# Two transformer layers on one core: compact value blocks, a reordered first group, and layer 0's scores taken bank by bank

## The chip, the cores and the metric

The kernel runs on one core of a Trainium2 chip. The metric is the time of the whole program on the device in microseconds; lower is better. All data starts in device memory and the result ends there.

## The reference, cut to what matters

`x` is 4 batches of 512 rows of width 128; the context has 77 rows per batch. There are 16 heads of width 8 in both cross-attentions.

```python
x = x + xattn0(layernorm(x), ctx, ctx, mask)   # softmax over 77 keys, mask fill -1e8, projections q k v o with biases
x = x + ffn0(layernorm(x))                     # attention over the 4 batches (4 heads), then 8 experts, top-1 gate, capacity 256
x = x + xattn1(layernorm(x), ctx, ctx)         # keeps the 32 largest scores of each row, softmax over them; v is ctx itself
x = x + ffn1(layernorm(x))                     # r * (relu(k)^2 @ Wv), inputs shifted by one row
# in both cross-attentions, for each head:
scores = q @ k.T / sqrt(8)
out = softmax(scores) @ v
```

## The kernel before

The 2048 rows of `x` are 16 tiles of 128 rows. The program has stages that follow one another on all engines:

1. Preparation. Weights and constants come in by DMA. Keys for both cross-attentions are projected (L925, L926) and spread into block-diagonal form: `kblk` holds, in each group of 32 partitions (four heads of width 8), four blocks of 77 columns, so that one matmul over 32 partitions gives the scores of four heads, 308 columns, one PSUM bank. Values are spread too: the 16 x 77 = 1232 pairs of head and key are cut into ten chunks of 128 rows, and `vblk[chunk]` is a 128 x 144 block, 128 columns for the output and 16 for the softmax denominators, zero except in the columns of the two or three heads that the chunk's rows belong to. ScalarE writes the transposed context sixteen times over (L415), TensorE multiplies each 128-column piece of it with all of Wv or transposes it (L937, L939), VectorE multiplies with a head mask (L627), twelve times for each layer. Then layer 1's mixing weights are made (L633 to L638).
2. Layer 0, cross-attention and feed-forward attention with gating, in four groups of four tiles (one of each batch). Each engine has its own program; all of them follow one list of step names, `GROUP_ORDER`, and each takes from it the steps that it has. The list is written out by hand. Steps of `attend` are of group j, steps of `among` of group j-1. Semaphores order the engines; an engine's queue runs strictly in its order. The first group also holds `w12a`, `w12b` (products w1 w2 of the eight experts, 64 TensorE records) and `b12` (64 records).
3. A hand-over, and then the 16 tiles one by one: experts, layer 1's query, top-32 on VectorE (L866, L877), weighing on GpSimd and ScalarE, the value product (L1168), layer 1's feed-forward. It is a software pipeline in the order of `TILE_ORDER`; value runs two tiles behind the top-k, mix three.

A tile of layer 0's cross-attention goes thus (names are those of the list, b is the tile in the group):
- `s` (L971, L974): four score matmuls, one for each bank, each on its own 32 partitions; then four more that add the mask row (65 partitions, bf16) to the four banks.
- `mx` (L671): one VectorE maximum over all four banks, 1232 columns.
- `sub` (L676): one VectorE subtraction from PSUM into `d0` in SBUF. The next tile's `s` waits for it.
- `exp` (L435): one ScalarE exponential from `d0` into `e0`, which scales by 1/sqrt(8).
- `ta`, `tb`, `tc` (L988): ten TensorE transposes, copied to SBUF by ScalarE (`ca` L440, `cc` L444, L445) and VectorE (`cb` L683).
- `v` (L998): ten value matmuls into one PSUM bank, fp32, which are 20 TensorE records; `nm` (L688, L691) divides by the denominators; `ot`, `oT`, `op` transpose and project (L1003, L450, L1007); `x` (L697) adds to the residual. `v` of a tile waits for `x` of the one before, since they share the bank.

In the list `hstats`, `hrstd`, `hnorm`, `hturn`, `hT`, `hq`, `hqT` are the layer norm of four tiles (L643, L646, L282, L653), its transposes (L951), and the query projection (L962). `q`, `qs`, `qk`, `dot`, `soft`, `wv`, `tot`, `res`, `ynorm` and `gate` are the feed-forward attention of the group before, mostly on VectorE. Steps for GpSimd in the list are `hrstd`, `bias`, `zrstd`, `zbias`, `xbias`, `yrstd`, `yaffine`, `ystore`.

SP's queue carries the input DMAs in order: context, weights, columns, mask, x, rows, biases, w1; and w2 only when the context area that it overwrites is free (L253).

## Time and profile before

| | us |
|---|---|
| median of 3 runs | 688.25 (688.17 to 688.58) |
| profiled execution, first to last instruction | 689.4 |
| PE busy | 455.3 (66%) |
| DVE busy | 512.7 (74%) |
| ACT busy | 291.1 (42%) |
| POOL busy | 263.1 (38%) |

The page gives for the profiled execution its span, and no time of its own around it. PE is TensorE's matmuls, PEld its weight loads, DVE is VectorE, ACT ScalarE, POOL GpSimd, SP the engine that issues most DMAs. The second part of the page is the span in 40 slices of 17.2 us; a digit is the busy share in tenths, PEclk the granted TensorE clock (9 is full):

```profile
PE   3759958747765777685678776775666748455445
...
DVE  3644446966956963759989999979889799999800
ACT  3002222223222232443656677774656547553342
...
PEclk9978977988897897766778888886887788665555
```

The waits and the chain of the page are read by stage, not for the whole, since the stages have different limits. "From start to start" below is how far apart two instructions of one engine begin; durations overlap, so it is often less than the duration.

### The profile page before, as it was taken

To read this page: it belongs to the slowest core of one execution; us is meant where nothing else is said; L and a number is where in the kernel's file an instruction comes from. 1 tells how busy PE (TensorE), PEld (TensorE's weight loads), DVE (VectorE), ACT (ScalarE), POOL (GpSimd) and SP (SyncE) were. 2 spreads that over 40 slices of the span, in tenths; PEclk is the share of its full clock that TensorE was granted. 3 is DMA by queue.
4 is the path that set the end of the run, shared out by engine and by line. 5 is a ranking of instruction groups with operands and counts; after the bars stand their busy time and mean duration, and the time that the engine had idled before them with its cause. 6 is when DMAs were issued, how large, how long until landed. Compare 5 with 4: busy or idle time off the path is not lost. (4 is left out here: it accounts for less than half of the span.)

```text
span 689.4 us, 11334 instructions
## 1 busy us (share of the span) xinstructions
PE 455.3 (66%) x2460; PEld 338.7 (49%) x2460; DVE 512.7 (74%) x3078; ACT 291.1 (42%) x789; POOL 263.1 (38%) x404
## 2 busy tenths in 40 slices
PE   3759958747765777685678776775666748455445
PEld 2727744544652664353445554553455436444334
DVE  3644446966956963759989999979889799999800
ACT  3002222223222232443656677774656547553342
POOL 4010030032023022332556765655546646645442
PEclk9978977988897897766778888886887788665555
DMA  8030000000000000000000000000000000000000
GB/s 323 9 122 1 1 0 1 2 0 2 0 1 0 0 0 1 0 0 1 0 1 1 6 5 5 6 1 4 6 1 4 5 4 1 4 4 6 4 4 8
DMA packets 3816, 9.42 MB, mean 14 GB/s; under 512 B 808, under 2 KB 2992, under 8 KB 3376
## 3 DMA queue, kind: packets, MB, share of 16 engines
q1 hardware_dynamic: 3616, 7.96, 3.1%
q10 hardware_dynamic: 144, 0.88, 0.3%
q14 instruction: 42, 0.34, 0.2%
q8 instruction: 14, 0.23, 0.1%
HBM read 7.79 MB, written 1.05 MB: 13 GB/s over the span
## 5 line engine op out<-in xcount | busy, mean ns | idle before, releaser
L866 DVE MAX8 top<-area_b 128x8 f32<-128x77 f32 x768 | 112.1, 228 | 0.0
L877 DVE MATCH_REPLACE8 area_b<-top,area_b 128x77 f32<-128x77 f32 x512 | 106.9, 229 | 0.0
L374 POOL TENSOR_TENSOR e<-area_b 128x1232 f32<-128x1232 f32 x16 | 44.7, 2797 | 43.2 <-issue 23.0
L1168 PEld LDWEIGHTS psM<-vblk,pT 128*128 128x128 f32 (+1 forms) x320 | 54.3, 241 | 9.3 <-issue 9.3
L1154 PE MATMUL psT<-consts,e 128*128 128x128 f32 (+1 forms) x160 | 33.2, 331 | 38.6 <-POOL e L374 25.6
L1168 PE MATMUL psM<-vblk,pT 128*128 128x144 f32 (+3 forms) x320 | 53.7, 336 | 0.0
L877 DVE MATCH_REPLACE8 area_b<-top,area_a 128x77 f32<-128x77 f32 x256 | 53.5, 233 | 0.0
L998 PE MATMUL psM<-vblk,pT 128*128 128x144 f32 (+1 forms) x320 | 48.7, 314 | 6.8 <-DVE x L697 6.2
L362 POOL TENSOR_TENSOR d<-area_a,mxc 128x1232 f32<-128x1232 f32 x16 | 36.0, 2248 | 41.3 <-DVEq L893 41.3
L998 PEld LDWEIGHTS psM<-vblk,pT 128*128 128x128 f32 (+1 forms) x320 | 46.2, 214 | 8.8 <-ACT pT L445 5.3
L282 POOL TENSOR_TENSOR rstd_m<-veps_m,expo 128x4 f32<-128x4 f32 x8 | 8.4, 1050 | 109.9 <-DVE veps_m L648 109.9
L866 DVE MAX8 top<-area_a 128x8 f32<-128x77 f32 x256 | 37.4, 226 | 16.7 <-issue 10.9
L515 ACT ACTIVATE consts<-psM,cur 128x128 f32<-128x128 f32 x128 | 38.2, 369 | 17.5 <-PE psM L1116 17.5
L1154 PEld LDWEIGHTS psT<-consts,e 128*128 128x128 f32 (+1 forms) x160 | 19.7, 160 | 50.5 <-POOL e L374 26.1
L877 DVE MATCH_VALUE_LOAD area_b<-top,area_b 128x8 f32 x512 | 44.2, 86 | 0.0
L1116 PE MATMUL psM<-w,y1T 128*128 128x512 f32 (+1 forms) x64 | 35.6, 647 | 6.3 <-ACT consts L515 6.1
L671 DVE TENSOR_REDUCE mx<-psS 128x16 f32<-128x1232 f32 x16 | 23.0, 1438 | 21.5 <-PE psS L974 21.5
L282 POOL TENSOR_TENSOR rstd_x<-veps_x,expo 128x4 f32<-128x4 f32 x4 | 4.1, 1025 | 90.6 <-DVE veps_x L648 90.6
L1124 PE MATMUL psM<-consts 128*128 128x128 f32 x288 | 38.1, 291 | 0.0
L1124 PEld LDWEIGHTS psM<-consts 128*128 128x128 f32 x288 | 37.1, 209 | 0.0
L435 ACT ACTIVATE e<-d 128x1232 f32<-128x1232 f32 x16 | 19.7, 1231 | 39.4 <-DVE d L676 39.4
L367 POOL TENSOR_TENSOR area_b<-area_a,mxc 128x1232 f32<-128x1232 f32 x16 | 36.0, 2248 | 0.0
(212 smaller groups left out, 1130.9 us busy)
## 6 DMA issues: line engine op xcount, KB each, us to landing
area_a<-in_w1T SPq DMA_DIRECT2D x1, 2048.0 KB, 14.7
area_b<-in_w SPq DMA_DIRECT2D x1, 2048.0 KB, 8.2
x<-in_x SPq DMA_DIRECT2D x1, 1024.0 KB, 9.4
out<-fin SPq DMA_DIRECT2D x16, 64.0 KB, 1.5
consts<-in_consts ACTq DMA_DIRECT2D x1, 862.0 KB, 5.0
weights<-in_weights SPq DMA_DIRECT2D x1, 836.0 KB, 6.5
rows<-in_rows SPq DMA_DIRECT2D x1, 576.0 KB, 11.3
ctx_sb<-in_ctxT SPq DMA_DIRECT2D x1, 154.0 KB, 4.7
```

What stands on the lines that cost most here:

```text
L362: e.tensor_tensor(dif[:], scores_sb[par][:], mxc[:, 0, :, None].broadcast_to([P, H, KEYS]), ALU.subtract)\
L367: e.tensor_tensor(cut, scores_sb[par][:], mxc[:, 1, :, None].broadcast_to([P, H, KEYS]), ALU.subtract)\
L374: e.tensor_tensor(p1.rearrange("p (h k) -> p h k", k=KEYS), ex1, cut, ALU.mult).then_inc(s["p_set"], 1)
L515: ins = e.activation(mparts[:, x_], psM0[:, at + (x_ - lo) * D:at + (x_ - lo + 1) * D], ACT.Copy, scale=cur[:, D + x_:D + x_ + 1])
L671: e.tensor_reduce(mx0.rearrange("p (g i) -> p g i", g=G), scores_ps, AX, ALU.max).then_inc(s["s_max"], 1)
L866: ins = e.max(top[:, r, h], (left if r else scores_sb[par])[:, h])
L877: ins = e.match_replace(left[:, h], top[:, r, h], (left if r else scores_sb[par])[:, h], GONE)
L998: ins = mm(psM0[:, 0:VW], pT[0:w, c], vblk0[0:w, b, c], start=(c == 0), stop=(c == NCH - 1))
L1116: mm(psM0[:, 0:(hi - lo) * D], y1T[:], w12[:, lo:hi].rearrange("p e n -> p (e n)"), start=True, stop=True)\
L1124: ins = mm(psM0[:, 0:D], ident, mparts[:, x_], start=False, stop=(x_ == E))
L1154: ins = tr(psT[0:w, 0, (c % 4) * P:(c % 4 + 1) * P], p1[:, c * P:c * P + w], ident)
L1168: ins = mm(psM1[:, 0:VW], pT1[0:w, c], vblk1[0:w, t // NJ, c], start=(c == 0), stop=(c == NCH - 1), skip_group_check=True)
```

## The change

- `vblk1` is made on the host and comes by DMA. `vblk0` has 27 columns a chunk for 144: three heads of 8 columns and a denominator column each (`FIRST` says which heads). It is made by 40 matmuls of 24 columns from the context, which comes three times over, and four VectorE maskings. The value products of both layers write 27 columns at the chunk's place in the bank.
- The first group of the list takes in the rest of the preparation: `masks`, `kblk`, `vb`, `vm`, `kblk1`, `wmix`, and w12 and b12 in eight pieces each. x comes in four DMAs, the first tile of each batch first; the weights in two parts.
- In every group of layer 0, `s`, `mx` and `e` are steps for each bank: one score matmul and its mask matmul, a negated maximum of four heads, four exponentials of 77 columns that read PSUM with the maximum as bias and write SBUF. `sub` and `d0` as its target are gone; `e0` alternates with the old `d0`. The factor 1/sqrt(8) is in the keys. A bank's scores wait for the exponentials of the same bank of the tile before.
- The list is a new one.

```diff
-VW = D + H
+VC = 3
+VE = HD + 1
+VW = H * VE
+VB = VC * VE
+REP = 3 * KEYS
+FIRST = [min(c * P // KEYS, H - VC) for c in range(NCH)]
+SHIFT = [c * P % KEYS for c in range(NCH)]
...
-    e.dma_start(cols[:], cols_d).then_inc(s["weights_in"], 16)
+    xt = x1.rearrange("p (b j) d -> p b j d", b=B)
+    xd = x.rearrange("p (b j) d -> p b j d", b=B)
+    e.dma_start(xt[:, :, 0], xd[:, :, 0]).then_inc(s["x_in"], 16)
+    e.dma_start(early[:], early_d).then_inc(s["early_in"], 16)
+    e.dma_start(cols[:], cols_d).then_inc(s["early_in"], 16)
     e.dma_start(mask_u8[:], mask.broadcast_to([P, B * KEYS]).rearrange("p (b k) -> p b k", b=B)).then_inc(s["mask_in"], 16)
-    e.dma_start(x1[:], x).then_inc(s["x_in"], 16)
-    e.dma_start(rows[:], rows_d.broadcast_to([P, sum(ROWS.values())])).then_inc(s["x_in"], 16)
+    e.dma_start(rows[:], rows_d.broadcast_to([P, sum(ROWS.values())])).then_inc(s["rows_in"], 16)
+    for j in range(1, NJ):
+        e.dma_start(xt[:, :, j], xd[:, :, j]).then_inc(s["x_rest"], 16)
     e.dma_start(b1T[:], b1T_d).then_inc(s["b_in"], 16)
     e.dma_start(b2[:], b2_d).then_inc(s["b_in"], 16)
+    e.dma_start(weights[:], weights_d).then_inc(s["weights_in"], 16)
     e.dma_start(w1T, w1T_d).then_inc(s["w1_in"], 16)
-    e.wait_ge(s["v_turned"], 2 * B * 3)
     e.dma_start(w2, w2_d).then_inc(s["w2_in"], 16)
...
-            def exp():
-                hold(e, s["s_sub"], u + 1)
-                hold(e, s["t_turned"], 3 * u)
-                e.activation(e0[:], d0.rearrange("p h k -> p (h k)"), ACT.Exp, scale=SCALE).then_inc(s["s_exp"], 1)
+            def exp(g):
+                def f():
+                    hold(e, s["s_max"], G * u + g + 1)
+                    if g == 0:
+                        hold(e, s["t_turned"], 3 * u - 3)
+                    for i in range(HG):
+                        h = HG * g + i
+                        ins = e.activation(e0s[b % 2][:, h * KEYS:(h + 1) * KEYS], scores_ps[:, g, i], ACT.Exp, bias=mx0[:, h:h + 1])
+                    ins.then_inc(s["s_exp"], 1)
...
-                        blk[:, :, None].broadcast_to([P, HG, KEYS]), ALU.mult).then_inc(s["kblk0_made"], 1)
-    for n in range(2 * B * 3):
-        v, b, g = (vblk0, vblk1)[n // (3 * B)], n // 3 % B, n % 3
-        lo, hi = 4 * g, min(4 * g + 4, NCH)
-        e.wait_ge(s["v_turned"], n + 1)
-        e.tensor_tensor(v[:, b, lo:hi, 0:D], psT[:, n % 2, 0:(hi - lo) * P].rearrange("p (c n) -> p c n", n=P),
-                        headmask[:, lo:hi, 0:D], ALU.mult).then_inc(s["v_masked"], 1)
-
...
-                hold(e, s["s_made"], u + 1)
-                hold(e, s["s_sub"], u)
-                e.tensor_reduce(mx0.rearrange("p (g i) -> p g i", g=G), scores_ps, AX, ALU.max).then_inc(s["s_max"], 1)
-
-            def subtract():
-                hold(e, s["s_max"], u + 1)
-                hold(e, s["s_exp"], u)
-                e.tensor_tensor(d0.rearrange("p (g i) k -> p g i k", g=G), scores_ps,
-                                mx0.rearrange("p (g i) -> p g i", g=G)[:, :, :, None].broadcast_to([P, G, HG, KEYS]),
-                                ALU.subtract).then_inc(s["s_sub"], 1)
+            def highest(g):
+                def f():
+                    hold(e, s["s_made"], G * u + g + 1)
+                    e.tensor_reduce(mx0[:, HG * g:HG * g + HG], scores_ps[:, g], AX, ALU.max, negate=True).then_inc(s["s_max"], 1)
+                return f
 
...
+            def masks():
+                e.wait_ge(s["mask_in"], 16)
+                e.tensor_copy(mask_f[:], mask_u8[:]).then_inc(s["mask_cast"], 1)
+                e.wait_ge(s["mask_cast"], 1)
+                e.wait_ge(s["constants_set"], 5)
+                for n, f in enumerate(fill_parts()):
+                    e.tensor_scalar(mrow[32 * n:32 * n + 1], mask_f[32 * n:32 * n + 1], -f, f, ALU.mult, ALU.add)\
+                        .then_inc(s["mrow_made"], 1)
+
+            def blocks():
+                e.wait_ge(s["k0_copied"], 1)
+                e.scalar_tensor_tensor(k0[:], k0[:], SCALE, mask_f[:], ALU.mult, ALU.mult).then_inc(s["k0_masked"], 1)
+                e.wait_ge(s["k0_masked"], 1)
+                e.wait_ge(s["consts_in"], 16)
+                for b in range(B):
+                    e.tensor_tensor(kblk0[:, b], k0[:, b, None, :].broadcast_to([P, HG, KEYS]),
+                                    blk[:, :, None].broadcast_to([P, HG, KEYS]), ALU.mult).then_inc(s["kblk0_made"], 1)
+
+            def values(b):
+                def f():
+                    e.wait_ge(s["v_turned"], b + 1)
+                    e.tensor_tensor(vblk0[:, b].rearrange("p c (i n) -> p (c i) n", n=VE)[:, :, 0:HD],
+                                    vbank[b % 2][:, 0:NCH * VC * HD].rearrange("p (n d) -> p n d", d=HD),
+                                    vmask, ALU.mult).then_inc(s["v_masked"], 1)
+                return f
...
     e.wait_ge(s["consts_in"], 16)
-    for n in range(2 * B * 3):
-        b, g = n // 3 % B, n % 3
-        e.wait_ge(s["ctx_rep"], b + 1)
-        if n >= 2:
-            e.wait_ge(s["v_masked"], n - 1)
-        for c in range(4 * g, min(4 * g + 4, NCH)):
-            dst = psT[:, n % 2, (c % 4) * P:(c % 4 + 1) * P]
-            if n < 3 * B:
-                ins = mm(dst, ctxrep[:, b, c * P:(c + 1) * P], Wt["wv0"], start=True, stop=True)
-            else:
-                ins = tr(dst, ctxrep[:, b, c * P:(c + 1) * P], ident)
-        ins.then_inc(s["v_turned"], 1)
...
 
-            def scores():
-                hold(e, s["h_qT"], j + 1)
-                hold(e, s["s_sub"], u)
-                for g in range(G):
+            def scores(g):
+                def f():
+                    if isinstance(u, int) and u == 0 and g == 0:
+                        e.wait_ge(s["kblk0_made"], B)
+                        e.wait_ge(s["mrow_made"], 3)
+                        e.wait_ge(s["constants_set"], 4)
+                    hold(e, s["h_qT"], j + 1)
+                    hold(e, s["s_exp"], G * u - G + g + 1)
                     mm(psS[:, g, 0:GW], q0T[32 * g:32 * g + 32, b], kblk0[32 * g:32 * g + 32, b].rearrange("p i k -> p (i k)"),
                        start=True, stop=False)
-                for g in range(G):
-                    ins = mm(psS[:, g, 0:GW], mones[:], mrow[:, b].rearrange("p i k -> p (i k)"), start=False, stop=True)
-                ins.then_inc(s["s_made"], 1)
+                    mm(psS[:, g, 0:GW], mones[:], mrow[:, b, None, :].broadcast_to([65, HG, KEYS]), start=False, stop=True).then_inc(s["s_made"], 1)
+                return f
 
...
-                    ins = mm(psM0[:, 0:VW], pT[0:w, c], vblk0[0:w, b, c], start=(c == 0), stop=(c == NCH - 1))
+                    ins = mm(psM0[:, FIRST[c] * VE:FIRST[c] * VE + VB], pT[0:w, c], vblk0[0:w, b, c], start=(c == 0),
+                             stop=(c == NCH - 1), skip_group_check=True)
                 ins.then_inc(s["pv_made"], 1)
 
...
-            def merged(n):
+            def spread(b):
                 def f():
-                    e.wait_ge(s["w1_in"], 16)
-                    e.wait_ge(s["w2_in"], 16)
-                    hold(e, s["w12_stored"], n)
-                    for x_ in range(4 * n, 4 * n + 4):
-                        for c in range(FC):
-                            ins = mm(psM1[:, (x_ % 4) * D:(x_ % 4 + 1) * D], w1T[:, c, x_], w2[:, c, x_], start=(c == 0), stop=(c == FC - 1))
-                    ins.then_inc(s["w12_made"], 1)
+                    if b == 0:
+                        e.wait_ge(s["k1_copied"], 1)
+                    if b >= 2:
+                        e.wait_ge(s["v_masked"], b - 1)
+                    for c in range(NCH):
+                        ins = mm(vbank[b % 2][:, c * VC * HD:(c + 1) * VC * HD], ctx_sb[:, b, SHIFT[c]:SHIFT[c] + P],
+                                 Wt["wv0"][:, FIRST[c] * HD:(FIRST[c] + VC) * HD], start=True, stop=True)
+                    ins.then_inc(s["v_turned"], 1)
                 return f
 
...
+            def merged(x_):
+                def f():
+                    if x_ == 0:
+                        e.wait_ge(s["w1_in"], 16)
+                        e.wait_ge(s["w2_in"], 16)
+                        e.wait_ge(s["v_masked"], B)
+                    if x_ == 4:
+                        e.wait_ge(s["w12_stored"], 1)
+                    for c in range(FC):
+                        ins = mm(psM1[:, (x_ % 4) * D:(x_ % 4 + 1) * D], w1T[:, c, x_], w2[:, c, x_], start=(c == 0), stop=(c == FC - 1))
+                    if x_ % 4 == 3:
+                        ins.then_inc(s["w12_made"], 1)
+                return f
+
...
 GROUP_AHEAD = dict(attend=0, among=-1)
-GROUP_ORDER = """hstats zstats hrstd hnorm hturn hT zrstd znorm zturn hq zT q0 qs0 hqT s0 w12a mx0 sub0 q1 s1 w12b qs1 q2
-exp0 w12c0 mx1 ta0 qs2 q3 tb0 sub1 ca0 qs3 cb0 qk0 tc0 s2 b12 bias qk1 dot0 qk2 dot1 cc0 qk3 dot2 mx2 dot3
-v0 nm0 exp1 w12c1 ta1 ca1 soft tb1 cb1 ot0 mexp oT0 tc1 op0 softw x0 wv0 cc1 sub2 v1 wv1 zbias tot0 wv2
-tot1 exp2 s3 wv3 tot2 ta2 nm1 ot1 tot3 tb2 mturn ca2 oT1 mx3 op1 cb2 b12c xbias x1 tc2 sub3 mTc proj res
-cc2 v2 yrstd exp3 ta3 nm2 ynorm ca3 ot2 tb3 cb3 tc3 oT2 yaffine op2 x2 cc3 v3 ystore yturn yT nm3 ot3 lg
-oT3 gdiff op3 x3 gexp gate""".split()
+GROUP_ORDER = """hstats masks zstats hrstd hnorm hturn kblk hT zrstd znorm zturn hq zT q0 qs0 hqT s00 s01 s02 s03 vb0 vb1 mx00 mx01 e00 mx02 mx03 vm0 q1 e01 s10 e02 vm1 vb2 kblk1 qs1 q2 mx10 s11 e03 vb3 vm2 qs2 ta0 mx11 s12 q3 e10
+ca0 tb0 mx12 s13 vm3 qs3 cb0 mx13 tc0  e11 cc0 qk0 wmix bias qk1 dot0 e12 qk2 dot1 v0 e13 wa0
+qk3 dot2 s20 ta1 nm0 ot0 dot3 mx20 s21 soft wa1 oT0 mexp op0 softw e20 ca1 s22 mx21 tb1 x0 mx22 s23 wa2 cb1 mx23 tc1 e21 cc1 wv0 wa3 w12c0 wv1 tot0
+e22 v1 wv2 tot1 e23 wa4 nm1 ot1 wv3 tot2 s30 ta2 mx30 oT1 s31 op1 tot3 mx31 wa5 wa6 e30 ca2 x1 s32 tb2 mturn mx32 s33 cb2 mx33 tc2 e31 wa7 w12c1 cc2 mTc
+zbias xbias proj res yrstd e32 v2 e33 bb0 bb1 bb2 ynorm nm2 ot2 ta3 yaffine oT2 tb3 op2 bb3 bb4 bb5 bb6 bb7 b12c ca3 cb3 tc3 x2 cc3 v3 ystore yturn yT nm3 ot3 lg oT3
+gdiff op3 x3 gexp gate""".split()
 
...
```

## Rows read from the trace of the kernel before

**Rows 1.** Busy time by stage: start:end, length, each engine's busy us, clock, DMA.
```profile
0.00:44.10 44.10, 22.92 (x124) 18.90 (x124) 24.66 (x61) 6.62 (x7) 8.39 (x25) 0.97 0.43 166
44.10:94.80 50.70, 44.19 (x314) 35.12 (x314) 17.31 (x26) 12.51 (x24) 1.69 (x4) 0.89 0.03 11
94.80:150.30 55.50, 39.13 (x222) 28.32 (x222) 40.43 (x100) 13.63 (x27) 10.83 (x15) 0.82 0.00 1
...
300.40:652.70 352.30, 228.01 (x1177) 168.55 (x1177) 326.21 (x2638) 204.09 (x590) 192.86 (x283) 0.76 0.01 4
652.70:689.40 36.70, 18.06 (x75) 15.35 (x74) 1.10 (x4) 11.58 (x33) 13.56 (x20) 0.59 0.02 5
```
**Rows 2.** Timeline of the preparation: start us, length us, what, idle before and releaser.
```profile
10.93 0.32 DVE L609 CAST mask_f<-mask_u 128x308 f32<-128x308 uint8 x1 [10.93 <-DMA mask_u<-in_mask]
11.28 4.96 DVE L614 TENSOR_SCALAR mrow<-mask_f 1x308 bf16<-1x308 f32 x12
...
27.61 2.69 PE L937 MATMUL psT<-weights,area_b 128*128 128x128 f32 x20 [0.21 <-DVE vblk L627]
...
42.88 1.11 DVE L653 TENSOR_SCALAR xn<-x,mv_x,rstd_x 128x128 f32<-128x128 f32 x4 [1.22 <-POOL rstd_x L282]
...
48.76 1.41 PE L971 MATMUL psS<-kblk,hT 32*128 32x308 f32 x8 [0.78 <-ACT hT L427]
```
**Rows 3.** Timeline of the first group: b12, and VectorE behind it.
```profile
65.56 7.15 PE L1030 MATMUL psM<-area_b,b1z 128*8 128x128 f32 x64 [0.77 <-ACT w L459]
...
75.40 0.26 DVE L688 RECIPROCAL rden<-psM 128x16 f32<-128x16 f32 x1 [9.13 <-PE psM L998]
```
**Rows 4.** Scores, second group: timeline rows, then L971's durations min/median/max in ns.
```profile
106.87 0.81 PE L1048 MATMUL psM<-weights,mT 128*128 128x384 f32 x2
...
117.31 0.80 PE L971 MATMUL psS<-kblk,hT 32*128 32x308 f32 x8
118.04 0.70 PE L974 MATMUL psS<-mrow,mones 65*128 65x308 bf16 x4
...
L971 PE MATMUL psS<-kblk,hT x128: 417/522/878, 48.8 to 240.6; 32*128 32x308 f32 x128
```
**Rows 5.** Other TensorE records: value product, 8-column records, value product in the tail.
```profile
118.57 2.62 PE L998 MATMUL psM<-vblk,pT 128*128 128x144 f32 x20
...
147.20 1.06 PE L1070 MATMUL psM<-weights,mT 128*128 128x8 f32 x8
...
673.14 4.28 PE psM L1168 x20
```
**Rows 6.** VectorE in the timeline, first and second group.
```profile
51.35 1.44 DVE L671 TENSOR_REDUCE mx<-psS 128x16 f32<-128x1232 f32 x1 [7.36 <-PE psS L974]
...
108.55 1.44 DVE L676 TENSOR_TENSOR d<-psS,mx 128x1232 f32<-128x1232 f32 x1
...
116.43 0.56 DVE L725 TENSOR_TENSOR qkv<-psM,rows 128x384 f32<-128x384 f32 x1 [0.45 <-PE psM L1048]
...
121.39 0.68 DVE L752 TENSOR_REDUCE sc<-prod 128x16 f32<-128x512 f32 x1
121.99 1.44 DVE L671 TENSOR_REDUCE mx<-psS 128x16 f32<-128x1232 f32 x1
...
141.33 1.12 DVE L653 TENSOR_SCALAR oo<-oo,mv_m,rstd_m 128x128 f32<-128x128 f32 x4 [0.64 <-POOL rstd_m L282]
...
146.12 0.26 DVE L688 RECIPROCAL rden<-psM 128x16 f32<-128x16 f32 x1 [2.88 <-PE psM L998]
```
**Rows 7.** ScalarE: timeline; two groups by line, with busy us and mean ns.
```profile
434.95 1.15 ACT L515 ACTIVATE consts<-psM,cur 128x128 f32<-128x128 f32 x4 [0.53 <-PE psM L1116]
...
L435 ACT ACTIVATE e<-d 128x1232 f32<-128x1232 f32 x16 | 19.7, 1231 | 39.4 <-DVE d L676 39.4
...
L515 ACT ACTIVATE consts<-psM,cur 128x128 f32<-128x128 f32 x19 | 5.7, 370 | 3.6 <-PE psM L1116 3.6
```
**Rows 8.** The copy that ends a tile's top-k: durations in ns, first and last start.
```profile
L889 DVE COPY mxc<-top x16: 174/175/175, 325.6 to 652.3; 128x16 f32<-128x16 f32 x16
```

More of the change, by code:

```diff
@@ L56, in fill_parts @@
     import numpy as np
-    rest = np.float32(MASK_FILL / SCALE)
+    rest = np.float32(MASK_FILL)
     out = []
@@ L705, in bias @@
                         e.tensor_tensor(b12[:], psM1[0:E, 0:D], b2[:], ALU.add).then_inc(s["b12_stored"], 1)
-                    steps["b12c"] = bias
+                    steps.update(masks=masks, kblk=blocks, wmix=mixed, b12c=bias, **{f"vm{b}": values(b) for b in range(B)})
                 return steps
@@ L1285 @@
     f32 = np.float32
-    head = np.arange(NCH * P) // KEYS
-    cols_of = np.arange(VW)
-    own = np.where(cols_of < D, cols_of // HD, cols_of - D)
-    headmask = (head[:, None] == own[None, :]).astype(f32).reshape(NCH, P, VW).transpose(1, 0, 2).reshape(P, -1)
+    row = np.arange(NCH * P)
+    head = np.where(row < SW, row // KEYS, H).reshape(NCH, P)
+    own = (head[:, :, None] == np.array(FIRST)[:, None, None] + np.arange(VC)).astype(f32)
+    ctx = a["ctx_1024"]
+    laid = np.zeros((NCH, P, B, VC, VE), f32)
+    for c in range(NCH):
+        for i in range(VC):
+            at = (FIRST[c] + i) * HD
+            rows_of = np.flatnonzero(own[c, :, i])
+            laid[c, rows_of, :, i, 0:HD] = ctx[:, row[c * P + rows_of] % KEYS, at:at + HD].transpose(1, 0, 2)
+            laid[c, rows_of, :, i, HD] = 1.0
     consts = np.concatenate([
@@ L1307 @@
         x=a["x"].reshape(NT, P, D).transpose(1, 0, 2),
-        ctxT=a["ctx_1024"].transpose(2, 0, 1),
+        ctxT=np.concatenate([ctx.transpose(2, 0, 1)] * 3, axis=2),
         mask=a["mask_BxS2_bf1"].view(np.uint8).reshape(1, B * KEYS),
-        consts=consts, weights=weights, cols=cols, rows=rows,
+        consts=consts, early=early, weights=weights, cols=cols, rows=rows, vblk1=laid.transpose(1, 2, 0, 3, 4).reshape(P, B, NCH, VB),
         b1T=a["L0_ffn_b1"].reshape(E, FC, P).transpose(2, 1, 0),
```

175 lines of the change are left out of this document (86 added, 89 removed).

## The prediction

> **What bounds the kernel now.** I read the page first, then the busy time by stage, then the timeline of each stage, then the waits. The busy shares over the whole run (VectorE 74%, TensorE 66%) mix five stages, and by stage [rows 1] the reader is to see five different kernels. From 0 to 44.1 us, preparation: no group of tiles has begun, VectorE has 24.7 us of work in it. From 44.1 to 94.8 the first group of layer 0: TensorE is busy 44.2 of 50.7 us, VectorE only 17.3, so TensorE's order is the bound. From 94.8 on three more groups of 55 us (one row stands for three), VectorE 40.4, TensorE 39.1: neither full, a chain of short steps at the ends and a VectorE queue without a gap in the middle. From 300.4 to 652.7 the sixteen top-k tiles, VectorE 326 of 352. Last a tail of 36.7 us.
>
> The top-k stage ends on VectorE: the copy that closes each tile's top-k comes from 325.6 to 652.3, fifteen intervals of 21.8 us [rows 8]. Of the change only the value matmuls and their normalisation reach into that stage, and these run beside the top-k. What is to be gained lies before 300 us and in the tail.
>
> **Preparation.** It builds both value blocks: 120 TensorE records that multiply or transpose a repeated context, and 24 VectorE multiplications, in a two-bank handshake. The steps of the first group come only after it: the layer norm's statistics and its power on GpSimd, normalising at 42.88, first scores at 48.76 [rows 2]. The change takes layer 1's blocks by DMA and moves everything else behind those steps. What then comes last? The mask: its transfer ends at 10.93 now [rows 2]. In the new queue 0.25 MB of x and 0.32 MB of weights stand ahead of it on SP, and the context is three times as wide on ACT's queue, in place of 0.99 MB ahead of it; I take 10 us (8 to 12). Behind it stand the cast 0.32 and three mask rows of 4.96/12 = 0.41 each, 1.6 us, then normalising 1.1: at 12.7 the first transpose can start. GpSimd's power needs the first quarter of x and the constants, both ahead of the mask, and I take it as done before. From normalising to first scores it is 5.9 us now (42.88 to 48.76), so first scores at about 17.5, 31 us earlier.
>
> **First group.** That is not 31 us for the run, since the work moved goes into the stage where TensorE has 6.5 us to spare. What it now does there:
> - layer 0's value blocks, 40 small matmuls of 24 columns, 80 records. A record costs 2.69/20 = 0.135 with 128 columns [rows 2] and 1.06/8 = 0.13 with 8 columns, drain included [rows 5]: columns buy little, the record is paced by its weight load. 9 to 11 us.
> - scores. Now the four head groups use rows 0-31, 32-63, 64-95, 96-127 of the array one after another in program order: eight records that last 417 to 522 ns each are through in 0.80 us, then four mask records in 0.70, 1.5 us [rows 4]. They run side by side. Bank by bank each one is followed by a 65-row mask matmul that shares its rows, and by a wait, so they go singly. A lone one is nearest to the 384-column pair, 0.81 x 308/384 = 0.65 us with drain, 0.53 without [rows 4]; with its mask record 0.65 to 0.8 per bank, 2.6 to 3.2 per tile. Bound below: if they still overlapped, 1.5. I take +1.3 per tile at the higher clock, 5.2 here.
> - minus the narrower value matmul: 20 records, 27 columns for 144, between 2.62 [rows 5] and 20 x 0.112 = 2.2: 0.3 per tile, 1.2.
> - w12 and b12 are the same records (b12: 64 in 7.15, [rows 3]), cut in pieces.
> Net +14 on TensorE (10 to 17). VectorE gains four masking steps (under 0.6 each by the 128x512 row, [rows 6]), the key block and the weight mix, about 6 us, hidden in its 33 idle [rows 1]. The pieces of b12 may fill waits: today VectorE and the chain stand 9.1 us behind its one block [rows 3]. I let 3 us of 6.5 be absorbed: 50.7 + 14 - 3 = 62, from 12.7 to 74.5. **First term: -20 us (-14 to -28).**
>
> A rule of the Trainium skill speaks against this step (TensorE: Matmul & The Clock Gate, Why this matters for your kernels): matmuls of few rows, laid on distinct 32-row groups, run concurrently, and four of them were measured 3.07 times as fast as singly. The trace agrees that they run together (417 ns records, eight in 0.80 us). By that factor the four would take 0.80 x 3.07 = 2.5 us singly, an estimate, +1.7 per tile and 1.5 us more in this group than I take; were the rule idle here, the first term would be 5 us better.
>
> **Later groups.** VectorE loses a subtraction of 1.44 and splits a maximum of 1.44 into four. A reduction of 512 elements takes 0.68 (0.60 to the next start), one of 1232 takes 1.44, so 1.06 ns an element; 308 elements come to 0.60 - 0.22 = 0.38 and four to 1.5, where one of 1232 costs 1.36 to the next start [rows 6]. Net -1.36 + 0.16 = -1.2 per tile, -4.8 per group. ScalarE: one exponential of 1.23 [rows 7] becomes 16 with a per-partition operand. Four of 128 columns with one take 1.15, 0.26 each from start to start, with 0.37 the length of one [rows 7]; 51 columns fewer at 1.0 ns (1.23/1232) gives 0.21, 0.83 per bank, 3.3 per tile, +2.1. Bounds 0.08 (77 columns at 1.0 ns, nothing fixed) and 0.37 (no overlap). ScalarE is busy 13.6 of 55 [rows 1], so +9 is covered as long as it keeps ahead. The chain of one tile is scores 2.6 at the lower clock (48.76 to 51.35, [rows 2, 6]), maximum 1.44, subtraction 1.44, exponential 1.23; after the change 1.3 + 0.45 for the first bank, then exponentials 3.3, while the next tile's banks follow: VectorE reaches its gap-free stretch some 3 us earlier, and has 2.3 less in it: -5. Against it: the new order puts nm2 behind ynorm, and ynorm waits for a power on GpSimd (0.64 idle at 141.33, with nm2 already done, [rows 6]); mTc stands behind e31 (0.8) on ScalarE. So v3, the transposes and the last addition are some 2 to 2.5 us later than they would be: half is given back. TensorE's +1.3 to +2.6 per tile takes room that is there (16 idle), if the low clock does not stretch it. I take -3 per group. **Second term: 3 x -3 = -9 (-20 to +6).**
>
> **Top-k stage and tail.** In the stage the narrow matmul is hidden by VectorE's queue: 0 (-1 to +2). In the tail one value product stands on the chain, 20 records in 4.28, most of them at the lower clock [rows 5]; at 0.21 a record (twice the 0.108 of a lone weight load's pace, as the 8-column row gives with its drain taken off) 0.6 goes. **Third term: -0.6 (-0.2 to -1).**
>
> **Sum.** -20 - 9 - 0.6 = -29.6. The profiled execution spans 689.4, 1.15 (0.2%) over the median 688.25 of the runs; the page gives no time around it, so I take the difference: 688.25 - 29.6, 658.5.
>
> **Rivals.**
> (a) The groups gain fully: VectorE's queue is the only bound, its saving 4.8 and the 3 us earlier start all count (-7 per group) and the first group packs well (-28): -28 - 21 - 1 = -50, 638. For it: VectorE is gap-free from 116.4 to 143.2 [rows 6]; v0 can start earlier. Against: nm2 behind ynorm.
> (b) TensorE takes over: scores cost +2.6 per tile in the stretches at the lower clock (half the rate) and each bank's wait holds the records queued behind it. Groups gain nothing (0 to +3 each), the first -14 to -17: 675 to 685, say 674 to 680. For it: 44.2 of 50.7 busy already.
> (c) Slower than before: the bank loop closes on itself. Scores of a bank wait for the exponentials of the tile before, on an in-order queue where transposes, in-projection and values stand behind. If scores (+2.6 at low clock) and exponentials (16 x 0.37 - 1.23 = +4.7) are both serial, a tile pays 7.3 and saves 2.9 and its narrow matmul 0.3: +4.1 each, +66 over 16, less 31 of preparation: 723. It decides from 31/16 = 1.9 net per tile. Against: ScalarE starts such an operation each 0.26 us today, 0.37 long, so they overlap.
> (d) No change: preparation's gain is eaten by the first group and the rest cancels; nothing in the rows adds up to that.
>
> **How the numbers follow.** Forecast (648 to 669) 0.52; (a) 630 to 648, 0.22; (b) 669 to 686, 0.17; (c) 0.07; (d) 0.02. Within 0.2%, about what a measurement tells apart, is (d). Range 638 to 673: it leaves out half of (a)'s far side, and of (b) what is above, and (c). Faster 0.91, same 0.02, slower 0.07.
>
> **What would show it.** First scores at 16 to 19.5; last x addition of the first group at 69 to 81; score records no longer overlapping, 2.6 to 3.2 a tile; exponentials 0.21 apart, 0.33 long; a group 52 us; value product 2.2 to 2.5; first to last closing copy of top-k unchanged at 326.7 us. It is wrong if groups are under 49 or over 55, or if the top-k spacing moves, which I hold to be fixed by VectorE alone.

## The result, and the profile after

The changed kernel takes **775.64 us** (median of 4 runs, 769.91 to 780.73) where the kernel before takes 688.41 (688.17 to 689.31) on the same chip: a ratio of **1.126, 95% interval 1.120 to 1.132**. I had forecast 658.5 and a range to 673. The profiled execution took 778.29 us, its span is 776.5. All these runs were in the faster of the chip's two states; one run of a kernel further below (c_old_narrow) was in the slower one and is left out.

Busy time by stage of the kernel after, columns as in [rows 1] (start:end, length; busy us of PE, PEld, DVE, ACT and POOL, each with its count of records; granted clock; DMA share; GB/s): the first group with what is left of the preparation, one of the three later groups, the top-k stage, the tail.

```profile
11.60:109.70 98.10, 91.53 (x394) 68.62 (x394) 20.24 (x49) 22.33 (x84) 4.64 (x7) 0.97 0.13 54
109.70:191.70 82.00, 71.11 (x222) 46.11 (x222) 37.98 (x108) 23.16 (x87) 10.82 (x15) 0.50 0.00 1
392.70:739.60 346.90, 244.87 (x1175) 186.90 (x1175) 319.84 (x2637) 202.79 (x590) 192.45 (x283) 0.70 0.01 4
739.60:776.50 36.90, 18.56 (x77) 15.83 (x76) 1.27 (x5) 11.54 (x33) 13.54 (x20) 0.50 0.02 6
```

Timeline of the first group, and a value product of the second (start us, length us, engine, line, operation, out<-in, shape; in brackets idle before and releaser):

```profile
16.38 1.36 PE L976 MATMUL psS<-kblk,hT 32*128 32x308 f32 x2 [0.87 <-ACT hT L440]
17.68 0.44 PE L978 MATMUL psS<-mrow,mones 65*128 65x308 bf16 x1
18.04 1.39 PE L976 MATMUL psS<-kblk,hT 32*128 32x308 f32 x2
18.15 0.48 DVE L658 TENSOR_REDUCE mx<-psS 128x4 f32<-128x308 f32 x1 [2.63 <-PE psS L978]
18.66 0.97 ACT L452 ACTIVATE e<-psS,mx 128x77 f32<-128x77 f32 x4 [2.42 <-DVE mx L658]
...
22.97 4.30 PE L1031 MATMUL psM<-early,ctx_sb 128*128 128x24 f32 x20
...
139.67 4.47 PE L1007 MATMUL psM<-vblk,pT 128*128 128x27 f32 x20 [0.53 <-ACT pT L464]
```

First scores come at 16.38, as forecast. The four banks of one tile then take from 16.38 to 22.97, 6.6 us, where the joint form of [rows 4] took 1.5 at the higher clock (at the lower one it takes 2.35, see c_old_wide0). The narrow value product takes 4.47 us for 27 columns, where the wide one took 2.62 for 144 [rows 5] at the higher clock and 4.28 at the lower. So the scores are slower at either level, and the value product is slow because of the level that it runs at.

Where the 87 us come from (each stage's length after, less that before): preparation -32 (first scores at 16.4, not 48.8), first group +47 (98.1 against 50.7), three groups +27 each, from the last group's end to the last closing copy of top-k 384.3 against 391.8, so -7.5, tail -0.2. Sum +87.

### The profile page after: what moved, and what is told of

The parts are those of the page before. It is cut to its first block and busy times, and to the rows that moved or that the text cites. A ratio compares the mean times of both kernels' runs of the same rounds, so it can differ in the third digit from the quotient of the medians.

```text
span 776.5 us, 11590 instructions
## 1 busy us (share of the span) xinstructions
PE 594.6 (77%) x2420; PEld 426.9 (55%) x2420; DVE 481.7 (62%) x3081; ACT 323.2 (42%) x1025; POOL 260.8 (34%) x396
## 5 line engine op out<-in xcount | busy, mean ns | idle before, releaser
L976 PE MATMUL psS<-kblk,hT 32*128 32x308 f32 x128 | 83.7, 751 | 0.9 <-ACT hT L440 0.9
L658 DVE TENSOR_REDUCE mx<-psS 128x4 f32<-128x308 f32 x64 | 30.6, 479 | 83.4 <-PE psS L978 83.2
L1007 PE MATMUL psM<-vblk,pT 128*128 128x27 f32 (+1 forms) x320 | 66.7, 377 | 7.2 <-ACT pT L464 6.3
L1007 PEld LDWEIGHTS psM<-vblk,pT 128*128 128x128 f32 (+1 forms) x320 | 65.6, 314 | 12.0 <-ACT pT L464 12.0
L1199 PEld LDWEIGHTS psM<-vblk,pT 128*128 128x128 f32 (+1 forms) x320 | 52.7, 253 | 9.6 <-issue 9.6
L1155 PE MATMUL psM<-mparts,consts 128*128 128x128 f32 x288 | 54.9, 373 | 0.0
L1155 PEld LDWEIGHTS psM<-mparts,consts 128*128 128x128 f32 x288 | 54.0, 289 | 0.0
L1199 PE MATMUL psM<-vblk,pT 128*128 128x27 f32 (+3 forms) x320 | 50.2, 317 | 0.0
L534 ACT ACTIVATE mparts<-psM,cur 128x128 f32<-128x128 f32 x128 | 37.9, 367 | 18.8 <-PE psM L1147 18.7
L976 PEld LDWEIGHTS psS<-kblk,hT 32*128 32x128 f32 x128 | 30.4, 294 | 25.6 <-issue 18.8
L452 ACT ACTIVATE d<-psS,mx 128x77 f32<-128x77 f32 x128 | 29.9, 333 | 26.9 <-DVE mx L658 26.9
```

Of the source, the lines that this page charges most:

```text
L452: ins = e.activation(e0s[b % 2][:, h * KEYS:(h + 1) * KEYS], scores_ps[:, g, i], ACT.Exp, bias=mx0[:, h:h + 1])
L534: ins = e.activation(mparts[:, x_], psM0[:, at + (x_ - lo) * D:at + (x_ - lo + 1) * D], ACT.Copy, scale=cur[:, D + x_:D + x_ + 1])
L658: e.tensor_reduce(mx0[:, HG * g:HG * g + HG], scores_ps[:, g], AX, ALU.max, negate=True).then_inc(s["s_max"], 1)
L976: mm(psS[:, g, 0:GW], q0T[32 * g:32 * g + 32, b], kblk0[32 * g:32 * g + 32, b].rearrange("p i k -> p (i k)"), start=True, stop=False)
L1007: ins = mm(psM0[:, FIRST[c] * VE:FIRST[c] * VE + VB], pT[0:w, c], vblk0[0:w, b, c], start=(c == 0), stop=(c == NCH - 1), skip_group_check= ...
L1155: ins = mm(psM0[:, 0:D], ident, mparts[:, x_], start=False, stop=(x_ == E))
```

## The experiments

The theories on record ahead of the first four runs were these: the scores that no longer run side by side are the cause, directly and through the clock (S); narrow value products pull the clock down (V); the waits of each bank and the new list are the cause (W). Theory A, ahead of the runs after them, is S and V together, acting through one clock. In a table first, since the texts lean on one another; all times in us, "before" is its run on the same chip, "group" the mean of the three later groups, clock the granted one in them:

```
run            time    before   first scores  first group  group   clock
before         688.3            48.8          46.0         55.2    0.83
after          775.6   688.4    16.4          93.3         81.9    0.51
b_banked       736.3   686.3    47.8          61.2         66.1    0.73
b_narrow       691.4   686.3    47.6          50.6         56.7    0.69
a_fused        698.6   686.3    16.3          65.6         64.5    0.63
a_wide         739.8   686.3    16.1          78.5         72.1    0.67
b_bank_nar0    761.4   689.4    48.1          63.9         73.0    0.60
a_fus_wide0    691.4   689.4    16.2          64.0         62.1    0.76
a_fw0_nm2      681.5   689.4    16.8          64.1         58.9    0.77
b_narrow1      692.0   689.4    47.5          46.1         56.3    0.82
c_old_wide0    675.2   688.0    17.3          62.8         56.5    0.82
c_old_narrow   682.8   688.0    18.2          68.2         56.9    0.69
```

("First group" is counted from the first scores here, to have one measure for all, and a stage's length is that of the profiled run.) The kernel after and the last two were timed several times; the others are single runs. Over thirteen runs on one chip the kernel before spread from 684.4 to 689.9, the kernel after over four from 769.9 to 780.7, and c_old_narrow over nine from 676.4 to 685.6. So a difference of 5 us between single times is not read, and one of 10 only where the stages of the traces bear it out.

### b_banked: the kernel before, with the mask matmul behind each score matmul

```diff
                         for g in range(G):
                             mm(psS[:, g, 0:GW], q0T[32 * g:32 * g + 32, b], kblk0[...], start=True, stop=False)
-                        for g in range(G):
                             ins = mm(psS[:, g, 0:GW], mones[:], mrow[...], start=False, stop=True)
```

> The kernel before with one thing altered: each score matmul is followed at once by the mask matmul of its own bank, so that the four 32-row matmuls no longer stand side by side in the program; waits, maximum, subtraction and exponential as before. Theory S (the single score matmuls are the cause, directly and through the clock): scores take 2.6 to 3.2 us a tile at the higher clock and 6.8 at the lower, the granted clock of the groups falls from 0.83 towards 0.55, groups of 70 to 80 us, 740 to 770 us in all. Theory V (the thin value matmuls pull the clock down): only the direct cost, 1.3 to 2.6 us a tile, clock of the groups unchanged near 0.83, 700 to 720 us. Theory W (the per-bank waits and the new list): 690 to 710.

Measured 736.34, 50 us above the kernel before, from deleting one line: the same eight matmuls in another order, and no new wait. It is theory S in kind, but less of it than expected: groups of 66 us where 70 to 80 were expected, the clock at 0.73 and not near 0.55. TensorE's timeline of b_banked, second group:

```profile
118.47 0.78 PE L971 MATMUL psS<-kblk,hT 32*128 32x308 f32 x2
119.19 0.30 PE L973 MATMUL psS<-mrow,mones 65*128 65x308 bf16 x1
119.42 0.78 PE L971 MATMUL psS<-kblk,hT 32*128 32x308 f32 x2
120.13 0.30 PE L973 MATMUL psS<-mrow,mones 65*128 65x308 bf16 x1
...
126.31 1.36 PE L971 MATMUL psS<-kblk,hT 32*128 32x308 f32 x2 [1.82 <-DVE d L676]
127.60 0.44 PE L973 MATMUL psS<-mrow,mones 65*128 65x308 bf16 x1
127.97 1.39 PE L971 MATMUL psS<-kblk,hT 32*128 32x308 f32 x2
```

It shows both levels of the clock. At the higher one a bank takes 0.95 us (118.47 to 119.42), 3.8 per tile; at the lower 1.66 (126.31 to 127.97), 6.6 per tile. The joint form takes 1.5 and 2.35. So the order alone costs TensorE 2.3 or 4.3 us per tile, by the clock, and the four groups, 47.7 us longer over 16 tiles, lie between: 3.0. A score pair by itself takes 0.72 here (118.47 to 119.19), four in turn 2.9; joint, all four are through in 0.73 (117.31 to 118.04, [rows 4]): a factor of 3.9. The Trainium skill (TensorE: Matmul & The Clock Gate, Why this matters for your kernels) gives 3.07 for four of 32 rows; the trace agrees that they run side by side, with the larger number. With a matmul over 65 rows between them, two of these pairs never overlap in the view above, and that is this case.

### b_narrow and b_narrow1: the kernel before, with narrow value products

```diff
-mm(psM0[:, 0:VW], pT[0:w, c], vblk0[0:w, b, c], ...)
+mm(psM0[:, FIRST[c] * VE:FIRST[c] * VE + VB], pT[0:w, c], vblk0[0:w, b, c, FIRST[c] * VE:FIRST[c] * VE + VB], ...)
```

(shortened; columns laid out head by head, 9 each; the blocks stay 144 wide in memory; b_narrow does both layers, b_narrow1 layer 1 only)

> The kernel before with one thing altered: the value blocks are laid out head by head with the denominator beside it, and the value matmuls of both layers stream 27 columns where they streamed 144; everything else, the making of the blocks included, as before. Theory V (thin value matmuls pull the clock down): the granted clock of the groups falls from 0.83 to 0.6 or less, value products take 4.3 us a tile there, groups of 65 to 75 us, 725 to 760 us in all. Theory S (scores): clock as before, 0.3 us less a tile, 683 to 688. Theory W (waits and list): the same 683 to 688.

Measured 691.39 against 686.28, a difference too small to be read. Both theories missed: V had 725 to 760, S a clock that stays. The granted clock of the three groups fell from 0.83 to 0.69, as V has it, but the three grew by 1.4 us on the mean and no more (the first, where TensorE has only 5 us idle, by 4.6): where TensorE has 16 of 55 us idle [rows 1], the slower records find room. In this one group it is busy 41.7 us at 0.68:

```profile
98.30:154.10 55.80, 41.71 (x222) 30.70 (x222) 40.41 (x99) 13.69 (x27) 10.83 (x15) 0.68 0.00 1
```

The narrow product brings the clock down, and here that costs the four groups 9 us in all. The top-k stage gave 7 back, which I had not forecast: from the groups' end to the last closing copy it took 384.5, not 391.8.

> The kernel before with 27-column value matmuls in layer 1 only. With both layers thin, the stretch from hand-over to last top-k went from 391.8 to 384.5 us, the groups got longer. Theory: the thin product shortens the chain that gives back the cut's buffer, three waits of 2.4 us of the copy that frees the scores, one an iteration, go away: 680 to 684 us, groups as before. Rival: the 7 us came from where the clock stood at the hand-over: 686 to 690.

Measured 691.97 against 689.38: no gain, where 680 to 684 was expected; the groups are those of before but for one of 58.4, and the stage behind them took 390.8. The narrow form in layer 1 alone does not bring what the two together brought.

### a_fused: the kernel after, with a tile's four score matmuls joint again

(shortened)

```diff
-    hold(e, s["s_exp"], G * u - G + g + 1)
-    mm(psS[:, g, 0:GW], q0T[32 * g:...], ...)       # one bank in each step
-    mm(psS[:, g, 0:GW], mones[:], mrow[...], ...)
+    if g > 0: return
+    hold(e, s["s_exp"], G * u)
+    for n in range(G): mm(psS[:, n, 0:GW], q0T[32 * n:...], ...)
+    for n in range(G): mm(psS[:, n, 0:GW], mones[:], mrow[...], ...)
```

> The changed kernel with one thing altered: the four score matmuls of a tile are issued together and the four mask matmuls after them, at the place of the first bank's step, once all exponentials of the tile before are done; maxima and exponentials stay bank by bank. Theory S: scores back to 1.5 us (2.6 at the lower clock), clock of the groups back to about 0.8, 650 to 690 us. Theory V: scores 2.6 us at the lower clock, 4.2 less a tile, and the clock stays near 0.5: 775 - 40 to 67 = 708 to 735. Theory W: 760 to 790, since the wait on the whole tile before is longer.

Measured 698.6, 77 us below the kernel after, between what S (650 to 690) and V (708 to 735) had. The bank-by-bank maxima and exponentials are all still there. The window row of one group:

```profile
81.80:144.30 62.50, 45.75 (x222) 34.35 (x222) 36.47 (x108) 22.90 (x87) 10.84 (x15) 0.64 0.00 1
```

TensorE's 71.1 busy us have become 45.75 with the same 222 records, and the clock rose from 0.50 to 0.64. Joint scores take away 77 of the 87 us, so most of what the change costs is in how the scores are issued.

### a_wide: the kernel after, with value blocks of 144 columns again

```diff
-vblk0 = sb("vblk0", [P, B, NCH, VB])
+vblk0 = sb("vblk0", [P, B, NCH, VW])              # zeros set first; vblk1 likewise
-mm(psM0[:, FIRST[c] * VE:FIRST[c] * VE + VB], pT[0:w, c], ...)
+mm(psM0[:, 0:VW], pT[0:w, c], ...)
```

> The changed kernel with one thing altered: the value blocks are 144 columns wide again with zeros outside the heads of a chunk, and the value matmuls of both layers stream 144 columns; scores bank by bank, list and preparation as changed (40 small VectorE writes and one fill of the block come in). Theory V: the clock of the groups returns to about 0.8, value products 2.6 us, 690 to 725 us. Theory S: clock stays near 0.5, value products 4.8 us at it, 775 to 790. Theory W: the same as S, 775 to 790.

Measured 739.81: **36 us less with five times as many columns to multiply**, mostly by zeros, and on VectorE 40 small masked writes where there were 4. V had 690 to 725, S 775 to 790; it lies between.

```profile
94.60:165.70 71.10, 59.05 (x222) 38.06 (x222) 37.73 (x107) 23.24 (x87) 10.82 (x15) 0.68 0.00 1
```

The clock is 0.68 where it was 0.50. This is the cleanest sight of the clock's part: TensorE doesn't wait less (12.0 us idle for 10.9), the same 222 records are through sooner, 59.05 busy us for 71.11, and the group is shorter by about as much, 11 us. So TensorE's records set the length of the group after. In the kernel before the narrow form had added 9 us to the four groups, here it adds 44 (the top-k stage gives 6 back). That the serial scores had used up the room on TensorE fits both, and the next run bears on it.

### b_bank_nar0: both in the kernel before

b_banked, with layer 0's value products narrow.

> The kernel before with both alterations in layer 0 alone: mask matmul behind each score matmul, and 27-column value matmuls (layer 1's value product keeps 144 columns). Alone the scores' order cost 50 us, the thin columns of layer 0 about 15 us in the groups (50.6, 55.9, 56.4, 57.7 us from 46.0, 55.5, 55.4, 54.8, and the hand-over). Theory A (both alterations act through one clock, so together they cost more than their sum): groups of 75 to 82 us as in the changed kernel with clock near 0.5, 760 to 790 us. Theory B (they add): groups of 66 to 70, 745 to 755. Theory W (waits and list make the rest of the changed kernel's groups): 735 to 750.

Measured 761.4, +72 us. The totals don't add up cleanly, since b_narrow also has layer 1 narrow; the four groups do: 71 us longer here, 48 in b_banked and 9 in b_narrow. That is about 14 more than the sum, as theory A says, and without any of the change's other parts. But the groups are 69.6 to 74.9 us and the clock 0.60, where it had 75 to 82 and 0.5.

### a_fus_wide0 and a_fw0_nm2: the kernel after without both, then with one step moved

a_fused, with layer 0's blocks wide and layer 1's narrow; the second also has

```diff
-... bb0 bb1 bb2 ynorm nm2 ot2 ...
+... bb0 bb1 bb2 nm2 ynorm ot2 ...
```

> The changed kernel with scores issued together and layer 0's value matmuls 144 columns wide, layer 1's left at 27. Theory A: the clock of the groups returns to 0.8 or more, first group 50 to 56 us from first scores, groups 50 to 55, hand-over to the last top-k as in the changed kernel (384): 16 + 54 + 3 x 53 + 384 + 37 = 640 to 660 us. If the new list and the sixteen exponentials have a cost of their own that the clock does not explain, the groups stay at 60 us or more, 675 to 700.

Measured 691.43, where theory A had 640 to 660 and its alternative 675 to 700. The groups are 62.1 on the mean, not 50 to 55: most of the clock is back (0.76) and yet each group is 7 us over the kernel before. So the bank-wise exponentials and the new list together do not pay, with joint scores they cost.

> As the kernel with joint scores and wide value matmuls in layer 0, and in the list nm2 stands ahead of ynorm. The prediction's step: nm2 behind ynorm costs 2 to 2.5 us a group, so three groups are 6 to 8 us shorter in all. Rival: the chain there is TensorE's (b12's pieces, values), and the move changes under 1 us a group.

Measured 681.54, 9.9 us less. The three groups gained 2.8, 5.2 and 1.6, while the first scores and the first group came out within 0.7 us of the other run's, so the difference of these two single runs lies where the step was moved. The order of nm2 behind ynorm is a price of 3.2 us a group. What is left shows in its timeline:

```profile
90.78 1.16 PE L985 MATMUL psS<-kblk,hT 32*128 32x308 f32 x8
...
92.22 1.64 DVE L662 TENSOR_REDUCE mx<-psS 128x4 f32<-128x308 f32 x4 [0.77 <-PE psS L988]
...
92.73 3.55 ACT L454 ACTIVATE e<-psS,mx 128x77 f32<-128x77 f32 x16 [2.44 <-DVE mx L662]
...
96.43 1.41 PE L985 MATMUL psS<-kblk,hT 32*128 32x308 f32 x8 [3.20 <-ACT e L454]
...
98.25 0.48 DVE L662 TENSOR_REDUCE mx<-psS 128x4 f32<-128x308 f32 x1 [3.93 <-PE psS L988]
```

The four banks are read by the exponentials, so the next joint scores wait until the sixteenth of them: TensorE stands 3.20 us, VectorE 3.93. Before, the banks came free at the end of a subtraction of 1.44 us [rows 6]. The subtraction that the change saves was also what freed the banks. (The joint form makes this wait. In the kernel after, where a bank waits for the exponentials of its own bank alone, the trace puts 2.2 us of TensorE's idle time down to them in the whole run, but there the scores take up to 6.6 us a tile.)

### c_old_wide0 and c_old_narrow: the new preparation alone

The kernel after with scores, maxima, subtraction and exponentials of the kernel before and its order of steps, in which the preparation's steps are set in; wide blocks in layer 0 and narrow in layer 1, or narrow in both.

```diff
-    for i in range(HG): ins = e.activation(e0s[b % 2][...], scores_ps[:, g, i], ACT.Exp, bias=mx0[:, h:h + 1])
+    e.activation(e0[:], d0.rearrange("p h k -> p (h k)"), ACT.Exp).then_inc(s["s_exp"], 1)
-GROUP_ORDER = "... s00 s01 s02 s03 vb0 vb1 mx00 mx01 e00 mx02 mx03 vm0 q1 e01 ..."
+GROUP_ORDER = "... s0 vb0 vb1 mx0 sub0 vm0 q1 s1 ..."
```

> The changed kernel's preparation (first scores at 16.5 us, compact values by host and by 24-column matmuls, w12 and b12 in pieces) with the scores of layer 0 as before: joint score matmuls, one maximum, one subtraction, one exponential from SBUF, 144-column value matmuls in layer 0, 27 in layer 1, and the list of before with the steps of preparation put in. Theory: what the chip lost in the changed kernel came from the scores bank by bank and the thin columns, and the preparation's 31 us are real. First group 52 to 60 us (46 before, plus 9 to 11 of value blocks), groups 55, hand-over to last top-k 385: 16.5 + 56 + 166 + 385 + 37 = 660, 652 to 668. Rival: the first group gives it all back (TensorE full there), 70 us or more from first scores: 675 and more.

Measured **675.18** (673.19 to 676.41) against 688.00: ratio **0.981 (0.978 to 0.984)**. It is faster than both kernels, and 15 us short of the 660 expected. The TensorE timeline of its first group says where about half of them are:

```profile
17.34 1.41 PE L982 MATMUL psS<-kblk,hT 32*128 32x308 f32 x8 [0.87 <-ACT hT L442]
18.69 1.21 PE L985 MATMUL psS<-mrow,mones 65*128 65x308 bf16 x4
19.69 4.30 PE L1038 MATMUL psM<-early,ctx_sb 128*128 128x24 f32 x20
23.81 4.44 PE L1038 MATMUL psT<-early,ctx_sb 128*128 128x24 f32 x20
...
30.53 4.30 PE L1038 MATMUL psM<-early,ctx_sb 128*128 128x24 f32 x20
34.65 4.44 PE L1038 MATMUL psT<-early,ctx_sb 128*128 128x24 f32 x20
...
43.68 0.80 PE L982 MATMUL psS<-kblk,hT 32*128 32x308 f32 x8
...
44.95 2.62 PE L1014 MATMUL psM<-vblk,pT 128*128 128x144 f32 x20
```

Joint scores take 2.35 us here (17.34 to 19.69). Eighty records of the value blocks take 17.5 us at 0.21 to 0.22 each, not 9 to 11; from about 40 us on the same engine works at the higher level (0.80 us for eight score records, as in [rows 4]). The preparation's gain of 31 us is here eaten by 17 in a first group of 62.8 for 46.0, and by 1.3 in each of the others; the top-k stage gives 4 back.

> The same with 27-column value matmuls in layer 0 as well. The kernel before lost 0.4 to 4.6 us a group by that, and its clock there went from 0.83 to 0.69. Theory: the same here, 5 to 15 us over the one with 144 columns, clock of the groups under 0.72. Rival: with joint scores the clock matters little and the shorter value product pays: equal or up to 4 us less.

Measured 682.83 (676.42 to 685.62), ratio 0.991 (0.988 to 0.994): 7.7 us above c_old_wide0, clock 0.69 against 0.82. The narrow block in layer 0 does not pay in either: 5.4 us are in the first group, where TensorE has 4 us idle, and only 0.4 in each of the others, where it has 15 and more.

## Why the prediction was wrong, point by point

The forecast was 658.5 and it was 775.6. **The step that failed is the price of TensorE's new forms at the clock of the kernel before**: the "+1.3 per tile at the higher clock", and behind it "takes room that is there (16 idle), if the low clock does not stretch it". It did: the scores came to 3.8 us a tile at the higher level and 6.6 at the lower, for 1.5, and the granted clock of the groups went from 0.83 to 0.51.

Undoing one part after another, the mean later group goes 81.9 (after), 64.5 (joint scores), 62.1 (and wide blocks), 58.9 (and nm2 first), 56.5 (and the old exponentials and list), 55.2 (before). In that order the joint form is worth 17.4 and the wide block 2.4. In the other one (a_wide first) the wide block is worth 9.8 and the joint form then 10.0. Only their sum, 19.8 of the 26.7, can be stated.

- Preparation: right. First scores at 16.4 for 17.5 (16 to 19.5).
- First group, -20 forecast with the preparation, +15 measured (-32 + 47). Three of its terms: value block records 9 to 11 us, measured 17.5; scores "2.6 to 3.2 us a tile", measured 3.8 at the higher and 6.6 at the lower clock, so 26 us for four tiles and not 10 to 13; and "minus 1.2" for the narrow product, which is plus 7.4 (4 x (4.47 - 2.62)). At the higher level the narrow product was as forecast, 2.42 for 2.2 to 2.5. The lone pair was nearly right (0.65 against 0.72 at the higher level); the mask record behind it, for which "0.65 to 0.8 per bank" left at most 0.15, adds 0.23. The large error is the other factor, 1.7 from one level to the other, and the level itself moved with what is run. I had the two levels before me: score records from 417 to 878 ns long stand in [rows 4], and the scores of the first tile took 1.41 us at 48.76 [rows 2] where those of the second group took 0.80. I took the higher one for the whole group.
- Later groups, -3 each forecast, +27 measured. Scores 6.6 for 1.5 and values 4.47 for 2.62 are +7.0 a tile, 28 of the 32 us by which TensorE's busy time grew; the other records are stretched by the clock too. The room that I counted on gave 5.5 us, for 16.4 idle went to 10.9 and no lower. VectorE's saving was there (40.4 to 38.0 busy) and bought nothing.
- The exponentials: right in their own price, short of what goes with it. The group line and source line of the kernel after (second: min/median/max in ns):

```profile
L658 DVE TENSOR_REDUCE mx<-psS 128x4 f32<-128x308 f32 x64 | 30.6, 479 | 83.4 <-PE psS L978 83.2
```

```profile
L452 ACT ACTIVATE e<-psS,mx x128: 316/326/377, 18.7 to 317.3; 128x77 f32<-128x77 f32 x128
```

  326 ns long and 0.21 apart (four in 0.97), as worked out; maxima 479 ns. What I did not price is that sixteen exponentials hold the banks for 3.55 us a tile (a_fw0_nm2). A gain of 3 us a group was forecast from this and the list; the step from 58.9 to 56.5 shows that the old form of both is 2.4 us better, and no run parts the two. VectorE's idle time before the maxima says who was late: 83.2 us behind the mask matmul L978.
- nm2 behind ynorm: "2 to 2.5 us later" a group, measured 3.2 in a_fw0_nm2. Right in kind.
- Top-k: I held the spacing to be fixed by VectorE alone. First to last closing copy is 321.8 us (417.8 to 739.6) for 326.7. A small miss, taken up below.
- Tail: 36.9 for 37.1, less than the 0.6 forecast. Its own numbers did not give 0.6: 20 records at 0.21 are 4.2 of 4.28. The narrow product there takes 4.31.
- Two slips without weight: 688.25 less 29.6 is 658.65 and not 658.5, and the stretch of VectorE called free of gaps holds the 0.64 at 141.33 [rows 6].
- The rivals: (c), the slower side, with a 0.07, was the nearest, and its point of decision (1.9 us net a tile) was passed by far; its mechanism was half right (scores at the low clock, serial), its other half (exponentials of 0.37 serial) was not needed, and its price of 66 was about half the 127 of the stages (47 + 80, with the work moved into the first group, 7.9 a tile). (b) named the low clock and let a group grow by 3 us at most. I gave the two 0.24 together; the rows with 1.41 us for a tile's scores should have made it more.

What stays open: why c_old_wide0's groups are still 1.3 us over those of before (52.9, 58.4 and 58.1 us, where before has 54.8 to 55.5); how much each of joint scores and wide blocks is worth by itself; and why narrow products in layer 1 alone (b_narrow1) shortened the stage behind the groups by 1 us when those in both layers (b_narrow) shortened it by 7, though layer 0's are over by then.

## What to carry to other kernels

Matmuls on few rows that run side by side did so here only while they stood next to each other in TensorE's queue: before splitting a batch of them for the sake of an earlier start, price the split form singly, with the matmul that comes between, and at the lower clock. A narrower moving operand hardly shortens a matmul that is paced by its weight load (2.62 to 2.42 us for 20 records), and it lowered the clock for all that stands around it; idle time on TensorE hides that, so the same edit adds 9 us to the groups of one kernel and 44 to those of another. And an operation that looks like a copy too many (a subtraction out of PSUM) may be what frees the banks early.

## What the runs showed of the hardware that I had not expected

**A TensorE that is seldom idle can be at its lower clock.** After, it has records in 71.1 of 82.0 us and is granted 0.50; before, in 39.1 of 55.5 and is granted 0.82. What it did in the one and not in the other is above: lone 32-row matmuls and products of 27 columns. With 144 columns for 27 the granted clock was 0.68. The first group after is the strongest case: TensorE has records in 91.5 of 98.1 us, and they show the lower level up to about 86 us and the higher one at 87. Right before the rise it worked through sixteen records of 128 columns:

```profile
80.09 1.39 PE L976 MATMUL psS<-kblk,hT 32*128 32x308 f32 x2
...
82.07 3.62 PE L1045 MATMUL psM<-area_b,area_a 128*128 128x128 f32 x16
...
87.48 0.78 PE L976 MATMUL psS<-kblk,hT 32*128 32x308 f32 x2
...
90.63 2.42 PE L1007 MATMUL psM<-vblk,pT 128*128 128x27 f32 x20 [1.01 <-ACT pT L464]
```

**Twenty records of 24 and of 27 columns take 4.30 and 4.47 us at the lower clock**, as 144 columns took 4.28 in the tail before [rows 5]: 0.21 to 0.22 each, whatever the columns. The median of the narrow product's weight loads is 333 ns at that level:

```profile
L1007 PEld LDWEIGHTS psM<-vblk,pT x320: 186/333/333, 50.4 to 348.4; 128*128 128x128 f32 x144, 80*128 80x128 f32 x16
```

**The top-k stage is not on VectorE alone.** The copy that a tile's top-k begins with (L885 before, L905 after; group line: busy us, mean ns, then idle before and its releaser):

```profile
L885 DVE COPY mxc<-top 128x16 f32<-128x16 f32 x16 | 9.6, 598 | 4.3 <-POOL area_b L367 2.6
```

```profile
L905 DVE COPY mxc<-top 128x16 f32<-128x16 f32 x16 | 3.2, 200 | 5.4 <-POOL area_b L383 3.7
```

Sixteen copies of a median of 0.175 us take 9.6, and one of them looks like this:

```profile
507.04 2.49 DVE L885 COPY mxc<-top 128x16 f32<-128x16 f32 x1
```

It is a wait, counted as busy, and the trace says for what: GpSimd was in its multiplication into `e`, which had started before the copy, and the copy ends 0.03 us after it.

```profile
506.70 2.80 POOL L374 TENSOR_TENSOR e<-area_b 128x1232 f32<-128x1232 f32 x1 [2.91 <-ACT area_b L559]
```

In all twelve traces 58 copies into mxc last over 200 ns, and 56 of them end about 0.03 us after an operation of GpSimd that had begun before them. All those over 1.5 us are held by this one multiplication. With the idle time before them the copies hold 13.9 us before and 8.6 after, 5.3 less, and the closing copies came closer by 4.9 (326.7 to 321.8).

Over the runs the sum goes roughly with the stage's length from the groups' end to the last closing copy. In the four kernels with wide products in layer 1 the sum is 13.1 to 13.9 and the stage 390.3 to 391.8 (before, b_banked, b_bank_nar0, a_wide). In the eight with narrow ones it is 7.9 to 11.5 and 384.3 to 390.8; the highest of these is b_narrow1, the run that narrows layer 1 and nothing else. So narrow products in this stage go with copies that meet GpSimd's multiplication less often, but by themselves they bring 1 us and not 7, and what brings the rest stays open.
